# A compact query on VectorE, spread to four heads by ScalarE and GpSimd, in a gated-attention kernel

## The reference

```python
q = (x @ Wq.T).reshape(b, l, H, K) * K ** (-0.5)
k = (x @ Wk.T).reshape(b, l, H, K)
v = (x @ Wv.T).reshape(b, l, H, V)
g = jax.nn.log_sigmoid(x @ Wg.T).reshape(b, l, H, K)
def step(S, inp):
    qt, kt, vt, gt = inp
    S = S * jnp.exp(gt)[..., None] + kt[..., None] * vt[..., None, :]
    yt = jnp.einsum('bhk,bhkv->bhv', qt, S)
    return (S, yt)
```

## Time and profile before

| | |
|---|---|
| median of 3 runs | 4213.58 us (4200.72 to 4215.24) |
| the profiled execution | 4204.48 us, of which the span of instructions is 4202.6 us |
| busy: TensorE, VectorE, ScalarE, GpSimd | 86%, 62%, 28%, 12% of the span |
| granted TensorE clock, mean | 0.909 of full speed |
| attention stretches of the four batches, first to last level update | 102.6, 407.1, 704.2, 1000.4 us, each some 150 us long |

### The profile page before, as it was taken

How to read it: one execution, slowest core, us unless ns; L and a number is a source line. 1 busy time by engine, 2 the same in 40 slices (tenths; PEclk the granted TensorE clock), 3 DMA queues, 4 the chain that set the end, 5 groups by cost and what they waited for, 6 DMA issues and landing times.

```text
span 4202.6 us, 38866 instructions
## 1 busy us (share of the span) xinstructions
PE 3598.4 (86%) x13526; PEld 2246.8 (53%) x13526; DVE 2610.6 (62%) x3722; ACT 1197.0 (28%) x1974; POOL 524.1 (12%) x419
## 2 busy tenths in 40 slices
PE   2887877878787999999999959898989898989988
PEld 1653644544545676676767725643564346434743
DVE  5876877877855556767776534464447444744463
ACT  1332432332313444333333322212221232113210
POOL 1002003012021111111111021120111011101100
PEclk9988988889898999999999978899889987998799
DMA  4212202202107676766666540122011300221011
GB/s 144 61 32 59 72 18 59 72 17 71 38 13 233 227 232 203 233 216 216 227 221 218 189 170 30 71 89 96 30 70 66 120 30 36 95 105 50 1 60 40
DMA packets 277843, 444.62 MB, mean 106 GB/s; under 512 B 52560, under 2 KB 189776, under 8 KB 265104
## 3 DMA queue, kind: packets, MB, share of 16 engines
q1 hardware_dynamic: 256768, 383.74, 27.8%
q0 software_dynamic: 20880, 58.40, 4.2%
HBM read 368.49 MB, written 97.70 MB: 111 GB/s over the span
## 4 chain that ended last, share of the span: by engine, by line
PE 62%; DVE 22%; DVEq 5%; ACT 4%; issue 3%; DMA 2%; POOL 1%; SPq 0%; ACTq 0%; POOLq 0%
PE bank L969 14%; PE bank L980 8%; PE bank L1211 5%; PE bank L1224 4%; PE bank L1230 4%; PE bank L787 3%; PE bank L1119 3%; PE bank L1078 3%; DVE sb_gla L1790 2%; PE bank L1097 2%; DVE sb_ratio L1765 2%; DVEq L1771 2%; PE bank L1155 1%; PE bank L767 1%; PE bank L764 1%
## 5 line engine op out<-in xcount | busy, mean ns | idle before, releaser
L969 PE MATMUL bank<-sb_xT,sb_work 128*128 128x256 f32 x3024 | 665.3, 380 | 1.6 <-issue 0.8
L969 PEld LDWEIGHTS bank<-sb_xT,sb_work 128*128 128x128 f32 x3024 | 576.0, 191 | 106.8 <-issue 31.3
L787 PE MATMUL bank<-sb_gla,sb_work 128*128 128x256 f32 x896 | 260.6, 444 | 113.9 <-DVE sb_work L1792 101.1
L980 PE MATMUL bank<-sb_work,sb_hT 128*128 128x512 f32 x756 | 355.4, 622 | 0.0
L787 PEld LDWEIGHTS bank<-sb_gla,sb_work 128*128 128x128 f32 x896 | 189.5, 219 | 176.9 <-DVE sb_work L1792 122.3
L767 PE MATMUL bank<-sb_hT,sb_work 128*128 128x512 f32 x384 | 182.0, 622 | 100.6 <-DVE sb_hT L1739 100.6
L1592 POOL DMA_INDIRECT sb_parts<-scratch_h,sb_small x126 | 140.7, 1117 | 982.8 <-DMA sb_small<-scratch_ids 963.3
L1224 PE MATMUL bank<-sb_parts,sb_small 128*128 128x512 f32 x512 | 244.2, 622 | 4.5 <-ACT sb_small L1536 4.5
L1230 PE MATMUL bank<-sb_parts,sb_small 128*128 128x512 f32 x512 | 230.8, 593 | 5.9 <-DVE sb_work L2303 5.9
L980 PEld LDWEIGHTS bank<-sb_work,sb_hT 128*128 128x128 f32 x756 | 147.7, 202 | 164.2 <-issue 164.2
L1211 PE MATMUL bank<-sb_work,sb_parts 128*128 128x512 f32 x512 | 232.7, 614 | 2.7 <-ACT sb_work L1547 2.7
(11 more groups left out here) (363 smaller groups left out, 6059.0 us busy)
## 6 DMA issues: line engine op xcount, KB each, us to landing
sb_work<-scratch_gu SPq DMA_DIRECT2D x63, 1408.0 KB, 7.7
sb_parts<-scratch_mx SPq DMA_DIRECT2D x16, 3072.0 KB, 10.2
sb_work<-moe_w SPq DMA_DIRECT2D x63, 512.0 KB, 5.1
scratch_y<-sb_work SPq DMA_DIRECT2D x63, 512.0 KB, 6.7
sb_parts<-scratch_fq SPq DMA_DIRECT2D x24, 1024.0 KB, 6.9
sb_work<-w_qkvg SPq DMA_DIRECT2D x64, 256.0 KB, 2.6
scratch_gu<-moe_w SPq DMA_DIRECT2D x32, 512.0 KB, 5.7
sb_parts<-fT SPq DMA_DIRECT2D x48, 256.0 KB
```

Source lines behind the costliest of these rows:

```text
L787: mm = pe.matmul(dst.rearrange("p (h n l) -> p h n l", h=HPC, l=size), kS[u % 2][:, k * P:(k + 1) * P], late[:, :, k, :, 1, :], start=True ...
L969: mm = pe.matmul(dst, egu[j % 3][:, which * NC + k, m * P:(m + 1) * P], xt[j % 2][:, k, :], start=(k == 0), stop=(k == NC - 1))
L980: mm = pe.matmul(bank(YB[s]), einter[j % 2][:, m * SLOTS + s * P:m * SLOTS + (s + 1) * P], edn[j % 3][:, m * D:(m + 1) * D], start=(m == 0 ...
```

## The change

VectorE's query update works on the compact `qa` (now two buffers), 128x256 elements. It is moved ahead of the wait for the level's scores and has a semaphore of its own, `g_updq`. For each level 1 to 6 the updated late columns are then copied into `qe`: ScalarE copies those of heads 0 and 1 (`spread_late`: two activations over 32 partitions and 256 columns), GpSimd those of heads 2 and 3 (two `tensor_scalar` over 128 partitions and 256 columns, multiplied by a 0/1 column, so that other heads' rows stay zero). TensorE's scores wait for both. `values_end` reads `qa` itself, so the four activations of `carry_over` that made `qc` go. GpSimd's `qa` and `qk` of the next unit stand behind its copies of levels 4 and 5.

```diff
-        g_qe = ev("g_qe", 1)
+        g_qe = ev("g_qe", NL)
+        g_qe2 = ev("g_qe2", NL - 1)
+        g_updq = ev("g_updq", NL)
...
+        def late_of(x, i, h, at):
+            r = slice(h * GK, (h + 1) * GK)
+            return x[r, at:at + T].rearrange("p (n a l) -> p n a l", a=2, l=1 << i)[:, :, 1, :]
...  TensorE, scores
                 if i:
                     pe.wait_ge(g_upd.sem, g_upd.at(u, i))
-                else:
-                    pe.wait_ge(g_qe.sem, g_qe.at(u, 1))
+                    pe.wait_ge(g_qe2.sem, g_qe2.at(u, i))
+                pe.wait_ge(g_qe.sem, g_qe.at(u, i + 1))
...  ScalarE
+            def spread_late(u, i):
+                act.wait_ge(g_updq.sem, g_updq.at(u, i))
+                act.wait_ge(g_s.sem, g_s.at(u, i))
+                for h in range(2):
+                    q = act.activation(late_of(qe[u % 2], i, h, h * T), late_of(qa[u % 2], i, h, 0), ACT.Copy)
+                q.then_inc(g_qe.sem, 1)
...  carry_over
-                act.wait_ge(g_upd.sem, g_upd.at(u, NL))
-                for h in range(HPC):
-                    r = slice(h * GK, (h + 1) * GK)
-                    act.activation(qc[r, :], qe[u % 2][r, h * T + P:(h + 1) * T], ACT.Copy)
...  GpSimd, for each unit
+                    for i in range(1, NL):
+                        pool.wait_ge(g_updq.sem, g_updq.at(u, i))
+                        pool.wait_ge(g_s.sem, g_s.at(u, i))
+                        for h in range(2, HPC):
+                            to, of = (x.rearrange("p (n a l) -> p n a l", a=2, l=1 << i)[:, :, 1, :]
+                                      for x in (qe[u % 2][:, h * T:(h + 1) * T], qa[u % 2]))
+                            q = pool.tensor_scalar(to, of, cst("own_head")[:, h * GK:h * GK + 1], None, ALU.mult)
+                        q.then_inc(g_qe2.sem, 1)
+                        if i == 4 and not last:
+                            queries(u + 1)
+                        if i == 5 and not last:
+                            same_step(u + 1)
...  VectorE, level
+                    dve.wait_ge(g_qe.sem, g_qe.at(u, i + 1))
+                    if i:
+                        dve.wait_ge(g_qe2.sem, g_qe2.at(u, i))
+                    late = qa[u % 2].rearrange("p (n a l) -> p n a l", a=2, l=size)[:, :, 1, :]
+                    tt(late, late, bcast(now2[:, :, 0], size), ALU.mult).then_inc(g_updq.sem, 1)
                     dve.wait_ge(g_s.sem, g_s.at(u, i + 1))
-                    late = qe[u % 2].rearrange("p (h n a l) -> p h n a l", h=HPC, a=2, l=size)[:, :, :, 1, :]
-                    tt(late, late, now2[:, :, 0].unsqueeze(1).unsqueeze(3).to_broadcast([P, HPC, n, size]), ALU.mult)
                     early = kS[u % 2].rearrange("p (n a l) -> p n a l", a=2, l=size)[:, :, 0, :]
                     tt(early, early, bcast(now2[:, :, 1], size), ALU.mult).then_inc(g_upd.sem, 1)
```

More of the change, by code:

```diff
@@ L394, in build @@
         qS, kS, aS = [[w(a + i * T, T) for i in range(2)] for a in (2048, 3072, 4096)]
-        qa, tots = w(5120, T), w(5632, T)
+        qa, tots = [w(5120, T), gla[:, 5120:5632]], w(5632, T)
         tot, at = [], 0
@@ L400, in build @@
         qe = [gla[:, i * 2048:(i + 1) * 2048] for i in range(2)]
-        qk, dv, qc = gla[:, 4096:4608], gla[:, 4608:5120], gla[:, 5120:5504]
+        qk, dv = gla[:, 4096:4608], gla[:, 4608:5120]
         Am = [w(6144, 2048), big[:, 0:2048]]
@@ L836, in values_end @@
                     mm = pe.matmul(bank(6)[:, (k + 1) * P:(k + 2) * P], Sbd[:, k * P:(k + 1) * P],
-                                   qc[:, k * P:(k + 1) * P], start=False, stop=(k == NT - 2))
+                                   qa[u % 2][:, (k + 1) * P:(k + 2) * P], start=False,
+                                   stop=(k == NT - 2))
                 mm.then_inc(g_y.sem, 1)
@@ L1307, in spread @@
                     r = slice(h * GK, (h + 1) * GK)
-                    q = act.activation(qe[u % 2][r, h * T:(h + 1) * T], qa[r, :], ACT.Copy)
+                    q = act.activation(qe[u % 2][r, h * T:(h + 1) * T], qa[u % 2][r, :], ACT.Copy)
+                q.then_inc(g_qe.sem, 1)
[4 more added lines that the diff above has]
+                    q = act.activation(late_of(qe[u % 2], i, h, h * T), late_of(qa[u % 2], i, h, 0), ACT.Copy)
                 q.then_inc(g_qe.sem, 1)
@@ L1344, in _ @@
                     u = b * NC + c
+                    spread_late(u, 1)
                     if c:
@@ L1348, in _ @@
                         exps(2 * NC * b + NC + c)
-                    if c + 1 < NC:
-                        for i in range(3):
+                    for i in range(3):
+                        spread_late(u, i + 2)
+                        if c + 1 < NC:
                             evacuate(u + 1, i)
-                            if c == 2 and i == 0:
-                                exps(2 * NC * b + NC + c)
-                    elif b == 0:
+                        if c == 2 and i == 0:
+                            exps(2 * NC * b + NC + c)
+                    if c == NC - 1 and b == 0:
                         act.wait_ge(wo_beta.sem, wo_beta.at(0, 1))
@@ L1362, in _ @@
                         exps(2 * NC * b + NC + c)
+                    spread_late(u, 5)
                     rectangles(u, 4)
@@ L1365, in _ @@
                         y_out(u - 1)
+                    spread_late(u, 6)
                     if c + 1 < NC:
@@ L1566, in _, with queries, same_step @@
                 pool.drain()
-                for u in range(b * NC, (b + 1) * NC):
+                def queries(u):
                     pool.wait_ge(g_evac.sem, g_evac.at(u, 3))
-                    if u:
-                        pool.wait_ge(g_qe.sem, g_qe.at(u - 1, 1))
-                    pool.tensor_tensor(qa, qS[u % 2], aS[u % 2], ALU.mult).then_inc(g_pool.sem, 1)
+                    if u >= 2:
+                        pool.wait_ge(g_y.sem, g_y.at(u - 2, 1))
+                    pool.tensor_tensor(qa[u % 2], qS[u % 2], aS[u % 2], ALU.mult).then_inc(g_pool.sem, 1)
+                def same_step(u):
                     if u:
@@ L1574, in _ @@
                     pool.tensor_tensor(qk, qS[u % 2], kS[u % 2], ALU.mult).then_inc(g_pool.sem, 1)
+                queries(b * NC)
+                same_step(b * NC)
+                for u in range(b * NC, (b + 1) * NC):
+                    last = u == b * NC + NC - 1
+                    for i in range(1, NL):
[10 more added lines that the diff above has]
+                            same_step(u + 1)
                 if b == 0:
```

1 line of the change is left out of this document (removed).

## The result

| | before | changed |
|---|---|---|
| median of 6 runs, us | 4210.00 | 4232.06 (4227.79 to 4238.80) |
| ratio, 95% interval | | 1.0055 (1.0040 to 1.0070) |
| span of the profiled execution, us | 4202.6 | 4230.6 |

The changed kernel is slower by half a per cent. Measured again later beside another kernel, it gave 4232.65 against 4211.86, ratio 1.0054 (1.0040 to 1.0068). The forecast was 4185, faster.

The account below looks back on a forecast made before the run. VectorE and TensorE, handing over at every level, were taken as the bound. Gains of 1.5 + 1.1 + 1.5 + 1.4 + 0.2 = 5.7 us a batch, 22.8 in all, gave 4181.7 to 4190.8, stated as 4185 us, range 4150 to 4225.

Parts of the forecast that it names:

- the walk: Step-by-step timing of a batch's four units, forecasting 1.5, 1.1, 1.5 and 1.4 us less in them.
- GpSimd's `qa` from 20.1 holds the scans 0.5 us: Second unit, 20.1 us after scores 0 end: `qa` follows the level-4 copies and delays VectorE's scans to 23.9.
- ScalarE as gate: Rival, no chance given: ScalarE's serial 4.85 us, already counted; if it were free, 1.2 us a unit more won.
- GpSimd's price: GpSimd's copies of late columns in each level: 0.5 us each, 1.0 the pair.
- the bound: Limits for one GpSimd copy: 0.31 us from a 128x256 memset, 0.63 from half a 128x512 two-input product.
- The lock: VectorE's two-SBUF-input operations and GpSimd's go one at a time; VectorE loses one copy, 0.5 us, a level.
- not in the way: Rival, chance 0.17: GpSimd's copies take 0.31 us or do not lock VectorE; -48 us, to 4156.
- The slower rival: Chance 0.18: GpSimd's copy between scores costs 1.27 us, +38 us, 4242; decides above 0.78 us a copy.
- slope: 1 us more per GpSimd copy moves a unit by 5 us: three levels' lock and two pairs' latency.
- ScalarE's serial chain: End of a unit: copies 0.8, `spread` 2.5 and level-5 rectangles 1.5 us follow one another before next scores 0.
- the last ratio piece: Last of VectorE's six ratio pieces, 742.96 + 2.44 to 747.25, taken as 1.7 us.
- The tail: After a batch's last unit: `carry_over` loses 2.1 us of ScalarE, but `states` waits for the averages; -0.2 us.

Follow-up runs that it names:

- qa_late: Changed kernel with GpSimd forming the next unit's `qa` behind its level-5 copies instead of in front: 4197.2 us, ratio 0.9963 against the kernel before.
- wait_kept: As qa_late, but GpSimd again waits for `values_end` of the unit before ahead of its level-5 copies, doing no work there: 4210.3 us, ratio 0.9987.
- qa_late_half: As qa_late, with head 3's late columns not copied, so GpSimd has one copy a level instead of two: 4165.7 us, ratio 0.9887.
- qa_late_tt: As qa_late, but GpSimd copies both heads with one `tensor_tensor` of 128x512 instead of two operations: 4233.2 us, ratio 1.0042.
- act4: As the changed kernel, but ScalarE copies all four heads' late columns and GpSimd none, keeping only its two products: 4195.1 us, ratio 0.9952.
- act4_order: As act4, with ScalarE's spread of the next unit's query in front of its level-6 copies, with its own semaphore: 4185.5 us, ratio 0.9935.

## Why the prediction was wrong

- **What bounds the kernel** was read rightly: VectorE and TensorE hand over at every level. VectorE's share fell as stated (33 to 27 us a unit), and the query update takes 426 ns. Scores 4 were to run at full pace; only three of sixteen do (1.96 to 1.97 us), the others take 2.8 to 3.8 us, since TensorE idles some 1.9 us for GpSimd's pair in the second unit and not 0.8.
- **The step that failed** is the walk at "GpSimd's `qa` from 20.1 holds the scans 0.5 us". It let `qa` start as soon as the level-4 copies were done and counted its work alone. Its wait for `values_end` of the previous unit, which is in the code and in the order of GpSimd's queue, was not in the walk, nor that the level-5 copies stand behind it. In the walk `qa` was done before these copies were due; in the trace it began 3.1 us after the level-5 pair could have, and held it for its own 1.4 us more. This costs what qa_late gives back: 35 us measured, of which the wait alone makes 13 (wait_kept). None of the rivals was this mechanism; "ScalarE as gate" was the right question put to the wrong queue.
- **GpSimd's price** was mis-sized: 0.92 to 1.39 us, mean 1.04, against 0.5, above both ends of the bound (0.31 to 0.63). Half of the pair gave back 31 us (qa_late_half). The bound came from other operations, and per element this one costs more than the two-input product (0.92 us for 256 elements against 1.27 for 512).
- **The lock** was charged 0.5 us a level for the copies and is not there: `tot` keeps its time. qa_late_tt shows what it would have cost. The rival "not in the way" was right in this half and wrong in "cheap".
- The two errors of size pull against each other, so the rest of the walk came out near by luck as well as by reading: with the queue mended, the stretches are 21.8 us shorter (forecast 22.0, without the tail), units 36.0, 34.9, 35.7, 34.6 against 35.4, 36.3, 36.0, 33.0. The second is 1.4 us better and the fourth 1.6 us worse than forecast, and only the sum agrees.
- **The slower rival** said that a copy above 0.78 us makes the kernel slower. It is above, and qa_late is faster all the same. Three of the 5 us a unit in its slope were the lock, which is not there. By its own sum the measured 1.04 us gives about 4225, near the 4232 of the changed kernel; that is luck, since it holds neither the wait nor the true cost of the lock. Its place (the pair stands between two scores) was right.
- **ScalarE's serial chain** was to be what the next scores 0 wait for. In the changed kernel it was not: scores 0 follow scores 6 without a gap at all twelve places, and in the second unit the rectangles of level 5 end at 789.0, 1 us before scores 6 do. The chain takes the 4.9 us that the walk gave it, but it is a gate only where the waits for GpSimd are gone (act4, act4_order). Of the prediction's signs of being wrong the first came: TensorE idles for GpSimd's copies at 32 places, 80 us in all.
- **A small misreading**: the last ratio piece, 742.96 + 2.44 to 747.25, is 1.85 us and not 1.7.
- **The tail**: from the end of scores 6 to the start of the last products (L888, before L880) 7.9 us against 8.4 in the third batch, -0.5; forecast -0.2. qa_late has the same 7.9 in all four batches. In the changed kernel's other three it is 8.9 to 9.1, since the averages' first products run at the lower clock there (3.75 us at a granted clock of 0.70 in the fourth batch, 2.74 at 1.00 in the third).

What stays open: outside the four stretches the profiled executions differ too, 3601.9 us before, 3614.2 changed, 3606 to 3622 in the variants, almost all of it in code that the change does not touch; 10 us of the changed kernel's 12 lie behind the last attention stretch. No run separates that from the scatter between executions of one kernel (4200.7 to 4219.8 for the kernel before), so of the measured loss of 22 us the 16 in the stretches are accounted for.

## What to carry to other kernels

When work is moved to an in-order queue, write out each wait of everything that stands in that queue, not only its durations: a wait that harms nobody by itself (`qa` for a free buffer) becomes costly when something urgent is put behind it. Look also for waits that the change itself brings in, as this one came with the reading of `qa` by `values_end`. Put the urgent work in front of what can wait; that one swap turned 0.5% slower into 0.4% faster here, and with three heads on ScalarE and the spread in front into 1.1% faster. Choose GpSimd's operation by what it holds up and not by its length alone.

## What the runs showed of the hardware

- GpSimd's `tensor_scalar` of 128x256 with a per-partition factor takes 0.92 us, 3.6 ns an element, while its `tensor_tensor` of 128x512 takes 1.16 us with broadcast inputs and 1.27 with two full ones.
- VectorE's operations with two SBUF inputs are held by GpSimd's `tensor_tensor` to its end (0.42 us becomes 1.26, in qa_late_tt), but hardly by its `tensor_scalar`: in the changed kernel the early keys stay at 0.42 to 0.43 us at all 112 places, and 88 `tot` begin during a copy and take no more than 0.42; four scans took 1.43 us for 1.20. The `tensor_scalar` is itself stretched to up to 1.39 us.
